# A written-out stage order changed: both down products in front of the head transposes, the norm of the delta stage moved, feed-forward pieces spread over the attention units, the first weight pack split

## What is computed

```
x += attention_a(norm(x))     # 16 softmax heads, latent keys and values, causal
x += moe(norm(x))             # 8 experts by low-rank additions, 2 chosen per token
x += attention_b(norm(x))     # per token: its 16 heads attend to each other, rotary angles
x += moe(norm(x))
x += delta(norm(x))           # gated delta rule over time, causal convolution before it
x += ffn(norm(x))             # GELU, 1024 hidden
x += attention_mq(norm(x))    # 16 query heads, one key and value head, causal
x += ffn(norm(x))
```

## Time and profile before

| | |
|---|---|
| median of 3 runs | 1475.29 us (1475.17 to 1475.62) |
| profiled execution | 1475.07 us, span 1473.3 us |
| mean granted clock of TensorE | 0.918 of full speed |
| TensorE busy | 1274.0 us, 86% |
| VectorE busy | 736.9 us, 50% |
| ScalarE busy | 420.7 us, 29% |
| GpSimd busy | 79.8 us, 5% |

### The profile page before, as it was taken

The page is one execution under the profiler, slowest core; times in us unless marked ns, Lnnn a source line. Parts: engine busy times, 40 slices in busy tenths (PEclk is TensorE's granted clock), DMA queues, the critical chain, the costliest instruction groups (busy, mean ns, idle before and its releaser), DMA issues.

```text
span 1473.3 us, 17475 instructions
## 1 busy us (share of the span) xinstructions
PE 1274.0 (86%) x6780; PEld 970.3 (66%) x6780; DVE 736.9 (50%) x1695; ACT 420.7 (29%) x909; POOL 79.8 (5%) x69
## 2 busy tenths in 40 slices
PE   5589997996898979888778899979779989898977
PEld 4468574764676869766566766747458677786755
DVE  4543277585337456334534334867834554653241
ACT  2523020221232333333442521212113323323341
POOL 0000000000110120000000000000001102100000
PEclk9999998998999869799998999989989998797997
DMA  9000000000000000000000000000000000000000
GB/s 378 26 1 0 0 1 0 1 1 0 1 1 1 1 1 1 2 1 8 1 8 1 0 1 1 1 0 1 0 1 1 1 1 1 1 1 1 0 8 8
DMA packets 3266, 16.98 MB, mean 12 GB/s; under 512 B 241, under 2 KB 2289, under 8 KB 2545
## 3 DMA queue, kind: packets, MB, share of 16 engines
q10 hardware_dynamic: 1008, 13.77, 2.3%
q1 hardware_dynamic: 2176, 2.10, 0.4%
HBM read 14.82 MB, written 1.05 MB: 11 GB/s over the span
## 4 chain that ended last, share of the span: by engine, by line
PE 66%; DVE 17%; ACT 8%; issue 7%; POOL 2%; DMA 1%; DVEq 0%; POOLq 0%; ACTq 0%
PE bank L638 62%; ACT scr L1207 4%; DVE scr L1701 2%; DVE scr L1700 2%; PE bank L645 2%; DVE stat L1465 1%; POOL rstd L1999 1%; DVE scr L1473 1%; DVE scr L1616 1%; DVE X L1458 1%; DVE negmax L1548 1%; ACT scr L1185 1%; DVE scr L1626 1%; DVE XnT L1858 1%; ACT XnT L1185 1%
## 5 line engine op out<-in xcount | busy, mean ns | idle before, releaser
L638 PE MATMUL bank<-pack,scr 128*128 128x512 f32 (+2 forms) x944 | 326.2, 495 | 8.1 <-ACT scr L1185 6.4
L638 PE MATMUL bank<-XnT,pack 128*128 128x256 f32 x1024 | 276.7, 415 | 18.7 <-ACT XnT L1185 11.6
L638 PEld LDWEIGHTS bank<-pack,scr 128*128 128x128 f32 x944 | 180.1, 197 | 128.4 <-issue 100.4
L638 PEld LDWEIGHTS bank<-XnT,pack 128*128 128x128 f32 x1024 | 208.7, 208 | 60.9 <-ACT XnT L1185 14.8
L638 PE MATMUL bank<-scr,pack 128*128 128x256 f32 x944 | 232.3, 387 | 3.4 <-DVE scr L1616 2.5
L638 PEld LDWEIGHTS bank<-scr,pack 128*128 128x128 f32 x944 | 181.6, 194 | 35.7 <-DVE scr L1616 5.7
L1626 DVE TENSOR_TENSOR scr<-bank,scr 128x256 f32<-128x256 f32 x112 | 47.2, 424 | 148.9 <-ACT scr L1254 147.2
L1185 ACT ACTIVATE scr<-bank 128x512 f32<-128x512 f32 (+7 forms) x112 | 50.8, 473 | 226.3 <-PE bank L645 125.6
L645 PE MATMUL bank<-pack,scr 128*128 128x128 f32 x232 | 41.4, 308 | 85.3 <-DVE scr L1473 38.4
L1254 ACT ACTIVATE scr<-bank 128x256 f32<-128x256 f32 x112 | 42.5, 384 | 247.3 <-PE bank L638 244.6
L1207 ACT ACTIVATE scr<-bank,negmax 128x256 f32<-128x256 f32 (+1 forms) x256 | 83.0, 442 | 95.7 <-DVE negmax L1548 92.7
(11 more groups left out here) (175 smaller groups left out, 1428.2 us busy)
## 6 DMA issues: line engine op xcount, KB each, us to landing
pack<-pack_dram ACTq DMA_DIRECT2D x1, 6408.0 KB, 17.8
pack<-pack_dram ACTq DMA_DIRECT2D x1, 2052.0 KB, 30.1
pack<-pack_dram ACTq DMA_DIRECT2D x1, 1595.0 KB, 23.2
pack<-pack_dram ACTq DMA_DIRECT2D x1, 1361.0 KB, 8.3
X<-x SPq DMA_DIRECT2D x4, 256.0 KB, 8.4
pack<-pack_dram ACTq DMA_DIRECT2D x1, 1024.0 KB, 19.9
out_dram<-X SPq DMA_DIRECT2D x4, 256.0 KB, 2.1
pack<-pack_dram ACTq DMA_DIRECT2D x1, 657.5 KB, 24.3
```

The costliest lines, as they stand in the source:

```text
L638: return pe.matmul(o, l, r, start=start, stop=stop, skip_group_check=True)
```

## The change

It rewrites the order in `program`, `middle`, `border`, `token_heads` and `experts`, splits three stages so that their parts can stand apart, and splits the first pack. In this order: 

1. Head places (4 of them): both down products of slot 1 stand before `head_out_t`; behind them lora_t, norm_x 3, lora, norm_t 3, router.

```diff
-            beside["down10"] = [("head_out_t", 0, s), ("head_out", 0, s), ("norm_x", 3, s)]
-            beside["down11"] = [("norm_t", 3, s)]
+            beside["down11"] = [("head_out_t", 0, s), ("head_out", 0, s)]
+            beside["lora_t"] = [("norm_x", 3, s)]
...
             summing[0] = False
             stage("lora_t", k, s)
+            others("lora_t")
...
             experts(stage, 0, b, token_heads(a))
+            stage("lora", 0, b)
+            stage("norm_t", 3, a)
             stage("router", 1, a)
-            stage("lora", 0, b)
             stage("spread_t", 1, a)
+            stage("top_exp", 1, a)
             stage("spread", 1, a)
```

```diff
-            experts(stage, 1, b, {0: [("norm_t", 4, a)], 1: [("delta_gate", 0, a)],
-                                  2: conv(a, 0) + [("delta_log", 0, a)], 3: conv(a, 1) + conv_silu(a, 0),
...
+            experts(stage, 1, b, {"f2": [("norm_t", 4, a)], 2: [("delta_gate", 0, a)],
+                                  3: conv(a, 0) + [("delta_log", 0, a)], 4: conv(a, 1) + conv_silu(a, 0),
...
-                    [("delta_decay", 0, b), ("delta_on", 0, a), ("delta_out_t", 0, a), ("delta_out", 0, a),
-                     ("norm_x", 5, a), ("delta_tok", 0, b), ("norm_t", 5, a), ("ffn_in", 0, (a, 0)),
-                     ("delta_qk", 0, b), ("delta_rows", 0, b), ("delta_mats", 0, b), ("delta_diag", 0, b),
-                     ("ffn_in", 0, (a, 1)), ("ffn_in", 0, (a, 2)), ("ffn_in", 0, (a, 3)),
+                    [("delta_tok", 0, b), ("delta_decay", 0, b), ("delta_on", 0, a), ("delta_out_t", 0, a),
+                     ("delta_out", 0, a), ("delta_sq", 0, b), ("norm_x", 5, a), ("delta_qk", 0, b), ("norm_t", 5, a),
+                     ("ffn_in", 0, (a, 0)), ("delta_rows", 0, b), ("ffn_in", 0, (a, 1)), ("delta_mats", 0, b),
+                     ("delta_diag", 0, b), ("ffn_in", 0, (a, 2)), ("ffn_in", 0, (a, 3)),
```

```diff
-            stream(stage, units(0, c), {-1: [("out_proj", 1, b), ("norm_x", 7, b)],
-                                        0: [("norm_t", 7, b)] + [("ffn_in", 1, (b, i)) for i in range(HT1 // 2)],
-                                        1: [("ffn_out", 1, b), ("norm_x", 0, d)]})
+            stream(stage, units(0, c), {0: [("norm_t", 7, b)] + ffn_in(1, b, 0, 1), 1: ffn_in(1, b, 2, 3),
+                                        2: half_(1, b, 0) + half_(1, b, 1) + [("norm_x", 0, d)]})
...
-            for other in (("scores", 0, (d, 0)), ("spread_t", 0, c), ("spread", 0, c), ("gates", 0, c)):
+            for other in (("scores", 0, (d, 0)), ("weights", 0, (d, 0)), ("spread_t", 0, c), ("top_exp", 0, c),
+                          ("values", 0, (d, 0)), ("scores", 0, (d, 1)), ("spread", 0, c), ("values_t", 0, (d, 0)),
+                          ("gates", 0, c)):
                 stage(*other)
```

```diff
-            stream(stage, units(1, d), {1: [("ffn_out", 1, c)]})
-            for other in [("out_in", 1, d), ("out_proj", 1, d), ("norm_x", 7, d), ("norm_t", 7, d)] + \
-                    [("ffn_in", 1, (d, i)) for i in range(HT1 // 2)] + [("ffn_out", 1, d)]:
+            stream(stage, units(1, d), {})
+            for other in [("out_in", 1, d)] + half_(1, c, 0) + [("out_proj", 1, d), ("norm_x", 7, d)] + \
+                    half_(1, c, 1) + [("norm_t", 7, d)] + ffn_in(1, d, 0, 1, 2, 3) + half_(1, d, 0) + half_(1, d, 1):
                 stage(*other)
```

```diff
             for s in range(B):
+                if s == S:
+                    sp.wait_ge(loaded[1], 16)
                 sp.dma_start(X[s][:, :, :], x_in[s].rearrange("(a p) d -> p a d", p=P)).then_inc(x_loaded[s], 16)
...
+            act.dma_start(pk[0][:, :], packs[0]).then_inc(loaded[0], 16)
+            act.dma_start(pk[1][:, :], packs[1]).then_inc(loaded[1], 16)
             act.dma_start(raw, masks).then_inc(masks_loaded, 16)
-            act.dma_start(pk[0][:, :], packs[0]).then_inc(loaded[0], 16)
             for s in range(S):
                 act.wait_ge(x_loaded[s], 16)
-            act.wait_ge(loaded[0], 16)
-            for g in range(1, len(packs)):
+            act.wait_ge(loaded[1], 16)
+            for g in range(2, len(packs)):
```

153 lines of the change are left out of this document (84 added, 69 removed).

## The result

The changed kernel takes 1457.4 us (median of 4, 1451.82 to 1458.43) against 1475.45 before: ratio 0.9853, 95% interval 0.9829 to 0.9877. Run again it gave 0.9856 (0.9831 to 0.9881). That is 22 us faster by the ratio (0.0147 of 1475) and 18 by the medians, where 43.3 were forecast; 1457.4 lies above the stated range. The direction was right, the size not. The profiled execution took 1458.43 us, its span is 1456.6, its mean granted clock 0.927 (before 0.918).

The account below looks back on a forecast made before the run. TensorE's work plus some 199 us of its idle time was taken as the bound. Terms 22.4 + 8.4 - 3 + 5.5 + 7 + 3 gave 43.3 us off 1475.07: 1431.8 us, range 1424 to 1441 (8 in 10: 1416 to 1449).

Parts of the forecast that it names:

- Head places: Four head-mixture waits: second down product goes in front, 5.6 us less idle each, 22.4 us faster (16 to 28).
- norm_t 4: Transposes before the delta stage, twice: moved behind two more x_first products, 4.2 us each, 8.4 us faster (4 to 13).
- GpSimd's order: Delta chain of sequence b, twice: squares now precede the norm, 1.5 us slower each, -3 us (-8 to +2).
- The passage: First to second pair of sequences: half of three waits totalling 11.5 us is won, 5.5 us faster (-2 to +10).
- B: Rival: each engine's order eats a third of the gain; 27 us faster in all, 1448 us; chance 0.20.
- C: Rival: small fills at head places and passage lower the granted clock, making the kernel slower, 1482 us; chance 0.03.
- The tail: Kernel's end: feed-forward halves of c leave d's attention stream to cover later waits, 7 us faster (3 to 8.5).
- The start: Kernel's start: smaller first pack and x held back bring the first projection earlier, 3 us faster (1 to 3.4).

Follow-up runs that it names:

- e10: Kernel before with only the new order of the four head places: 0.9890 of the kernel before.
- e9: Changed kernel with the whole middle delta chain back in the old order: 0.9860 of the kernel before, where the changed kernel has 0.9856.
- e16: Kernel before with the new start and the new order of the middle delta chain, nothing else: 1.0026 of the kernel before.
- e2: Changed kernel with the passage from sequences a, b to c, d back in the old order: 0.9795 of the kernel before.
- e13: Changed kernel with every stage order undone, so only the start is new: 1.0005 of the kernel before.
- e15: Kernel before with the new start and the new passage between the sequence pairs, nothing else: 1.0037 of the kernel before.
- e7: Changed kernel with 9 useless 128x512 products in the 10.35 us wait before norm_t 5 of each pair's first sequence: 0.9892 of the kernel before.
- e8: Kernel before with 8 useless 128x512 products in the 7.73 us wait of each head place, nothing moved: 0.9998 of the kernel before.

## Why the prediction was wrong

**Head places, 22.4 us.** The mechanism was right: wait 1.7 instead of 7.7 us, the normalised rows hidden behind lora. The step that failed is "5.6 us less per place, with the clock taken as it is". Idle time fell by 3.9 us at place 1 and by 10.7 in the whole kernel (e10), where the term has 22.4, as I counted two of ScalarE's three copies, had two waits for VectorE 0.3 us too short and missed the 0.98 us behind the place. And the clock cannot be taken as it is: it had been low over a wait, and is now low over work. Alone the four places are worth 16 us, at the low end of the term's own bounds.

**norm_t 4, 8.4 us.** The 5.26 us went; the bank wait came as 2.93 in place of 1.22, 1.7 us more where 1.6 were charged; behind it 0.9 us more. In the change it is worth 14 us, alone nothing or less, as the old head places beside it cost 5 to 8 us a pair in the delta stretch. The failed part is to give it one value at all.

**GpSimd's order, -3 us.** Right that it adds idle time, low on the amount (6.1 us a place, not 2 to 4), and right that the clock gives it back, which it does nearly whole: +1 and -3 us measured (e9, e16), neither clear of zero.

**The passage, +5.5 us.** The worst step: the sign. I took half of three waits as gain and did not follow what each filler left behind. The three waits fell by 6.8 us and new ones of 6.2 came, and the clock dropped to 0.89: the work at the lower level grew by 10.6 us against before, by 9.4 against e2 and by 9.5 from e13 to e15. Undone, it gives 9 us: the kernel is then 30 us faster than before, where the forecast without this term has 38. So of the 22 us that are missing by the ratio this one term is 14, and 8 remain for the others. Of the rivals B comes nearest, which had the passage at nothing; C named the passage as a place where the clock could fall, and that much of it came true.

**The tail, 7 us.** Undone 7 us slower; right as a size, as far as the interval tells. The out-projection ran at full clock, as forecast. The traces give 3.0 us against before, with a feed-forward half at the lower level, and 6.6 in the second one, where that half ran at full clock too. **The start, 3 us.** Wrong: the first projection comes 0.8 us earlier and not 3.3, as ScalarE's own DMA issues, which I had not followed, hold its table load; alone the new start shows no gain (e13).

**The sum.** Taken out one by one, head places, norm_t 4, chain, passage and tail are worth 30, 14, 1, -9 and 7 us, together 42 or 43: that this is what was forecast is luck. Put in alone, the first four are 16, -5, -3 and -5 and the start -1 (the tail alone was not measured). The change gave 21. So adding terms failed, beside the passage. The delta stretch shows it: in one and the same order it takes 53.0 or 60.6 us, in the old one 54.7 or 59.9, by the clock, and in the traces it is the order of two stages ahead of it that decides. How a change at 370 us sets the clock at 500 is not settled. The fills (e7, e8) show idle time to be part of it; that small products bring the clock down without a pause is seen in a trace, and no run tests it.

## What to carry to other kernels

Where the granted clock is well under 1, read idle time and busy time at the lower level apart, stretch by stretch. A wait taken out from under the lower clock can give less than its length, as at head place 1, where 3.9 us of wait gave 1.6, because the drop of the clock stayed and came to lie over work; a wait added there can cost nothing, as in the delta chain. Single edits of a few us don't add in such a kernel: measure the combination, and leave parts out of it one by one, as here where leaving out the passage gave 9 us more. Take two traces of one kernel before you explain a few us by a stretch: here they differed by 3.7 us in the tail alone.

## What was not expected of the hardware

TensorE can be at the lower level with no pause: 10.00 of 10.00 us busy at a mean clock of 0.68, most of it in products of 64 columns (e7). Filling waits with useless products of 128 x 512 took 7 us off the low time of the delta chain and nothing off its length. And executions of one kernel can differ early and late and be alike between: two traces of the changed kernel are apart by 1.8 us one way at 148 us and 1.0 the other way at 415, and from there to 1395 that distance stays within 0.3 us. The delta stretch takes 53.0 us in all seven traces that have the new head places, norm_t 4 and chain and no more done to them, whether it begins at 480.9 or at 491.5 us.
